# A recurrence step on VectorE as four whole instructions, and attention row transfers in another order on SyncE's queue

## The reference

```python
# layer 0, attention
scores = jnp.einsum('bhqd,bhkd->bhqk', q, k) / math.sqrt(HD)
attn = jax.nn.softmax(scores, axis=-1)
out = jnp.einsum('bhqk,bhkd->bhqd', attn, v)
# layer 1, the recurrence: one step for each token
def step(S, inp):
    q_t, k_t, v_t, g_t, b_t = inp
    S = S * jnp.exp(g_t)[..., None, None]
    mem = jnp.einsum('bhk,bhkv->bhv', k_t, S)
    delta = (v_t - mem) * b_t[..., None]
    S = S + jnp.einsum('bhk,bhv->bhkv', k_t, delta)
    o_t = jnp.einsum('bhk,bhkv->bhv', q_t, S)
    return (S, o_t)
```

## Time and profile before

| | us |
|---|---|
| median of 3 runs | 982.09 |
| lowest and highest | 980.87, 983.06 |
| profiled execution | 984.33 |
| its span in the trace | 982.5 |
| stretch of the attention groups in it | about 42 to 165 |
| steps of the recurrence in it | 544.4 to 679.3 |

### The profile page before, as it was taken

One profiled execution on the slowest core, in us unless ns is written; L12 is line 12 of the kernel. 1 busy time (PEld: TensorE's weight loads), 2 busy tenths in 40 slices (PEclk: granted clock), 3 DMA queues, 4 the chain that ended last, 5 costly groups with the idle time before them and its releaser, 6 DMA issues.

```text
span 982.5 us, 11403 instructions
## 1 busy us (share of the span) xinstructions
PE 780.4 (79%) x3600; PEld 508.9 (52%) x3600; DVE 636.3 (65%) x1522; ACT 287.5 (29%) x529; POOL 274.4 (28%) x250
## 2 busy tenths in 40 slices
PE   5876999879999999989503876453868699999983
PEld 4321333657777777744301322121345389999973
DVE  4785993654444444468998899998966734334335
ACT  2444776423334333335300543331011000000000
POOL 3630000211222222212744035334410124434410
PEclk9987999879999999999856887775978799999995
DMA  8691000001111111302200000000001289999945
GB/s 271 171 188 28 2 3 33 20 21 41 48 45 35 48 48 48 114 1 97 96 0 0 1 0 1 0 1 0 0 1 43 99 295 343 343 335 346 344 152 169
DMA packets 36405, 94.13 MB, mean 96 GB/s; under 512 B 4910, under 2 KB 17766, under 8 KB 35526
## 3 DMA queue, kind: packets, MB, share of 16 engines
q1 hardware_dynamic: 32262, 83.19, 26.4%
q0 software_dynamic: 3648, 9.97, 2.8%
q10 hardware_dynamic: 448, 0.39, 0.2%
HBM read 82.21 MB, written 12.12 MB: 96 GB/s over the span
## 4 chain that ended last, share of the span: by engine, by line
PE 54%; DVE 32%; issue 6%; DMA 5%; ACT 1%; SPq 1%; ACTq 0%; POOL 0%; DVEq 0%; POOLq 0%
PE psum L1243 14%; PE psum L1488 8%; PE psum L1498 7%; PE psum L1254 7%; DVE arena L1963 3%; DVE arena L1976 3%; PE psum L1143 3%; PE psum L1122 3%; PE psum L1132 3%; DVE arena L1954 2%; DVE arena L1967 2%; DVE small L1649 2%; DVE arena L309 2%; DVE arena L1923 2%; DMA max_scratch<-max_sb 1%
## 5 line engine op out<-in xcount | busy, mean ns | idle before, releaser
L1243 PE MATMUL psum<-xr,wr 128*128 128x512 f32 x600 | 159.3, 416 | 1.1 <-DVE arena L1798 1.1
L1243 PEld LDWEIGHTS psum<-xr,wr 128*128 128x128 f32 x600 | 116.3, 195 | 25.6 <-issue 1.3
L607 POOL TENSOR_TENSOR wr<-ring,wr 128x512 fp32r<-128x512 f32 (+1 forms) x50 | 54.3, 1105 | 198.9 <-ACT wr L810 198.9
L1649 DVE TENSOR_REDUCE small<-psum 128x1 f32<-128x512 f32 x128 | 80.9, 684 | 21.5 <-PE psum L1122 20.8
L1488 PEld LDWEIGHTS psum<-arena 128*128 128x128 f32 x700 | 83.3, 191 | 4.1 <-issue 1.6
L1488 PE MATMUL psum<-arena 128*128 128x128 f32 x700 | 84.0, 274 | 1.4 <-ACT arena L1010 1.1
L1498 PE MATMUL psum<-arena 128*128 128x256 f32 x350 | 81.8, 379 | 1.9 <-DVE arena L2162 1.9
L2151 DVE TENSOR_SCALAR arena<-psum,arena 128x256 f32<-128x256 f32 x35 | 16.9, 484 | 102.0 <-PE psum L1498 102.0
L1050 PE MATMUL psum<-sel,identb 128*128 128x512 bf16 x164 | 45.9, 421 | 46.2 <-DVE arena L1931 46.2
L1761 DVE TENSOR_TENSOR hid<-hid,psum 128x512 f32<-128x512 f32 x50 | 34.4, 688 | 69.0 <-ACT hid L816 69.0
L1254 PE MATMUL psum<-hr,wr 128*128 128x512 f32 x300 | 76.4, 391 | 0.2 <-DVE hr L1736 0.2
(11 more groups left out here) (364 smaller groups left out, 1339.2 us busy)
## 6 DMA issues: line engine op xcount, KB each, us to landing
arena<-in_w1u SPq DMA_DIRECT2D x35, 642.5 KB
arena<-in_w1d SPq DMA_DIRECT2D x35, 640.0 KB
ring<-in_w SPq DMA_DIRECT2D x25, 384.0 KB, 3.1
part_scratch<-arena SPq DMA_DIRECT2D x12, 256.0 KB, 2.0
arena<-z_scratch SPq DMA_DIRECT2D x8, 384.0 KB, 6.6
arena<-part_scratch SPq DMA_DIRECT2D x9, 256.0 KB, 12.9
qkv_scratch<-arena SPq DMA_DIRECT2D x4, 512.0 KB, 2.6
arena<-qkv_scratch SPq DMA_DIRECT2D x4, 512.0 KB, 4.0
```

The lines of the kernel that those rows point to most:

```text
L607: pool.tensor_tensor(wr0[:, k, LO, part], ring0[:, k, part], wr0[:, k, HI, part], ALU.subtract).then_inc(s["w0_lo"], 1)
L1243: ins = pe.matmul(bank[2 * b + m][:, :], wr0[:, k, w, lo:lo + P], xr[:, x, f, half(b)], start=(f == 0 and (w, x) == PARTS[0]), stop=(f == ...
L1649: dve.tensor_reduce(nm[:, g % 2, at16:at16 + 1], full("scores", n), AX, ALU.max, negate=True).then_inc(s["bank_free"], 1)
```

## The change

SyncE: row set 1 is issued ahead of the stores of pair 1 instead of behind them. Row set 3 is issued behind the maxima's two transfers of g = 1 instead of ahead of them. Row set 2 keeps its place behind the wait for pair 1. VectorE: each stage of a step is one instruction over both halves, with one semaphore `scan` instead of `scan_lo` and `scan_hi`; its count per step stays 4. The other engines wait for `scan` alone. The data, their places and the arithmetic of each element are the same.

```diff
             q_rows(sp, 0, half(1), rows_in(0, 1))
-            parts_out(1)
-            for t in range(1, NH // HG):
-                if t == 2:
-                    sp.wait_ge(s["parts_out1"], 16 * 6)
+            def all_rows(t):
                 k_rows(sp, t, slice(0, TOK), rows_in(t, 0))
                 q_rows(sp, t, slice(0, TOK), rows_in(t, 0))
+
+            all_rows(1)
+            parts_out(1)
+            sp.wait_ge(s["parts_out1"], 16 * 6)
+            all_rows(2)
...
                      max_dram.rearrange("(h j t) q -> h j (t q)", h=2, j=HG))
+                if g == 1:
+                    all_rows(3)
...
-                for x in range(2):
-                    if x == 0:
-                        dve.wait_ge(s["u_in"], n + 1)
-                    dve.wait_ge(own[x], 4 * n + 1)
-                    dve.tensor_reduce(fixed[:, x], pa[:, n % 2, x], AX, ALU.add).then_inc(own[x], 1)
...
+                dve.wait_ge(s["u_in"], n + 1)
+                dve.wait_ge(own, 4 * n + 1)
+                dve.tensor_reduce(fixed, pan, AX, ALU.add).then_inc(own, 1)
```

## The result

| | before | after |
|---|---|---|
| median of 5 runs each (us) | 982.09 | 991.71 |
| lowest to highest | 980.87 to 983.06 | 988.12 to 993.03 |
| profiled execution | 984.33 (span 982.5) | 991.71 (span 989.9) |
| TensorE's second scores of group 1 begin | 81.58 | 73.01 |
| the transposes behind attention begin (L1213, now L1214) | 166.65 | 159.30 |

The change made the kernel slower: the ratio after to before is 1.0095, with a 95% interval of 1.0073 to 1.0117. Both parts did what their diffs say, with opposite signs: attention and what follows it reach the recurrence 9.6 us earlier, the recurrence takes 19.4 us more, and 2.4 us come back behind it. That makes the 7.4 by which the spans differ. The medians differ by 9.6, because the profiled execution of before lay 2.2 above its median and that of after lies on it.

What follows compares the result with a forecast made beforehand. Neither PE (54% of the chain) nor DVE (32%) was taken to bound the whole kernel; VectorE sets the recurrence's time. Recurrence +23.0 - 4.3 = +18.7, attention -9.3, together +9.4 on 982.09: 991.5 us, range 977 to 1001.

Steps and rivals of the forecast that it cites:

- the main case: Whole kernel: recurrence +18.7 us, attention -9.3, so 991.5 us; chance 0.62.
- The plain step: Recurrence with GpSimd idle: a step takes 2.18 us instead of 1.82, +23.0 us for 64 steps.
- The waits for GpSimd: Recurrence beside GpSimd: VectorE's products wait 0.44 us each, 14.1 us in all instead of 18.4, so -4.3.
- The threshold: Recurrence beside GpSimd: GpSimd wants the memory again at 0.63 us, VectorE asks at 0.67, so GpSimd comes first.
- the first rival: Recurrence: GpSimd comes too late and VectorE never waits, +4.6 us there, kernel 977.4 us; chance 0.13.
- the second's: Recurrence: the gap is 0.04 before reduces too, VectorE asks at 0.60, ahead of GpSimd; kernel 968.5 us; chance 0.10.
- Attention: First exchange: the store of maxima lands right behind set 2, TensorE goes on at 72.7, -8.9 us; with clock -9.3.
- The lower bound of -11.9: Attention's largest gain: the store meets an empty queue, landing within about 1.4 us, and TensorE avoids the lower clock.
- TensorE's clock: Attention behind the wait: the shorter wait may spare TensorE the lower clock, a gain of 0 to 2.1 us, 0.4 taken.
- Row set 3: Attention: issued around 73 to 76, in by about 85; may delay the next exchange a us or so, costed at nothing.
- my own range: Whole kernel: the forecast's range, with L1955, attention and the waits at their bounds, 983 to 998 us.
- The third rival: Recurrence: a wait costs nothing, a step's four paces are 1.56 us, kernel 945.5 us; chance 0.03.

Runs made afterwards that it cites:

- the eleventh kernel: The changed kernel with each of GpSimd's products replaced by a write of one element; one run of 980.12 us.
- the fourth kernel: The changed kernel with the two waits in the other order ahead of both reduces; 985.31 us, ratio 1.0029.
- the fifth kernel: The changed kernel with each GpSimd product waiting for the one ahead and ScalarE's copies of sums and queries moved later; 982.08 us, ratio 0.9988.
- the second kernel: The kernel before with the whole instructions alone, SyncE's order as before; 999.44 us, ratio 1.0157.
- ninth kernel: The changed kernel with waits swapped ahead of both reduces, GpSimd's products made late, and the first 19 steps in halves; 966.88 us, ratio 0.9859.
- the eighth kernel: The kernel before with row set 1 alone moved ahead of the stores of pair 1; 979.33 us, ratio 0.9968.

## Why the prediction was right

The time came out at 991.71 for a forecast of 991.5, and the main case was the one that happened. By its steps:

- **The plain step** was 2.21 for 2.18. The reduces took 0.453 for 0.44, L1955 0.60 for 0.59, L1964 0.426 for 0.41; the gaps were 0.103 and 0.034 for 0.11 and 0.04. Over 64 steps that is +24.8 for +23.0. That the 0.11 belongs to the order of the two waits, and not to the copy from PSUM behind which it had been read, is shown by the two swaps.
- **The waits for GpSimd** were 154.2 - 64 x 2.208 = 12.9 us for 14.1 (12.5 by the eleventh kernel), the lengthening of a product 0.42 to 0.43 for 0.44. The recurrence as a whole came to 154.2 for about 153.
- **The threshold was the weak step.** "Wants the memory again at 0.63" was read from two record starts after GpSimd had come from idle. In a run of products the time is 0.57. The outcome was right, and safer than I thought: the margin was 0.10, not 0.04. But the first rival's price point was wrong, and so was the second's reasoning: with gaps of 0.04 everywhere VectorE would still have lost, at 985.3 (the fourth kernel) and not at 968.5. What that rival priced was reached only by making GpSimd late (966.4).
- **Attention** came at -8.6 for the wait, forecast -8.9, but by another road. The row sets were quicker than worked out: the six stores of pair 1 landed 0.6 us apart, the last one 1.1 behind the fifth, at 56.63 and not "by 60.9 at the latest", and set 2 was in at 66.93, not between 69 and 71.9. The store of maxima then met an idle queue, and by the prediction's own words it should have landed within 1.4. It took 3.05, with this in the windows (columns as in the next point):

```profile
68.00:69.00 1.00, 1.00 (x9) 0.33 (x10) 1.00 (x3) 0.54 (x2) 0.00 (x0) 1.00 0.10 24
69.00:70.00 1.00, 1.00 (x9) 0.11 (x2) 1.00 (x2) 0.77 (x1) 0.00 (x0) 1.00 0.00 1
```

  The 24 GB/s in the first of the two are the store's 8 KB and the 16 KB of the instruction packet. A store that waits for row loads and one whose last packets stand behind an instruction packet gave the same time by chance; the first was my mechanism, the second was what happened. The lower bound of -11.9, with a store of 1.4 and the clock kept, is the case of the fifth kernel, and it goes a little beyond: the second value matmuls end at 76.64 there, 12.7 earlier than before.
- **TensorE's clock** was forecast to give back 0.4 and took 0.9 instead: from TensorE's going on to the end of the second value matmuls it is 8.66 us, before 7.76. The granted clock is 0.50, the 1.2 GHz level, when TensorE goes on. The windows (start to end, length; busy us and count of PE, PEld, DVE, ACT, POOL; granted clock, DMA share, GB/s), first before, then after:

```profile
81.58:85.58 4.00, 4.00 (x15) 1.04 (x15) 1.98 (x3) 2.05 (x2) 0.00 (x0) 0.50 0.00 0
85.58:87.58 2.00, 2.00 (x14) 0.53 (x7) 0.69 (x1) 0.86 (x2) 0.00 (x0) 0.82 0.00 0
```

```profile
73.01:77.01 4.00, 4.00 (x15) 1.04 (x15) 1.98 (x3) 2.05 (x2) 0.00 (x0) 0.50 1.08 207
77.01:79.01 2.00, 2.00 (x11) 0.43 (x4) 0.41 (x1) 0.60 (x1) 0.00 (x0) 0.50 1.00 152
79.01:81.01 2.00, 2.00 (x10) 0.60 (x12) 1.78 (x5) 1.53 (x2) 0.00 (x0) 0.83 0.80 172
```

  Before, the full clock is back some 4.7 us after TensorE goes on, after the change some 6.7. The clock had fallen 8.9 us ahead of TensorE's going on before, and 0.16 ahead of it now, so that less of the slow stretch passed while TensorE was idle. The second value matmuls end at 88.29 + 1.05 before and 80.62 + 1.05 now, 7.7 earlier where the start was 8.6 earlier. At L1214 7.35 are left.
- **Two stretches with the same code** came out shorter in the profiled execution. The recurrence begins 9.6 earlier, 2.2 more than at L1214, and the stretch behind it gave 2.4 on top. The change made neither of them. From the transposes behind attention to the recurrence the 14 profiled executions take 375.5 to 379.2 us, those with SyncE's order of before 375.5 to 377.8. Behind the recurrence the 12 other kernels take 302.6 to 304.2, the second kernel with its whole instructions 302.6; the 300.9 of the changed kernel stands alone. So the first is scatter between single executions. The second lies 1.7 under the lowest of the others, over code that the change didn't touch, and most likely is scatter too; only one execution of the changed kernel has a trace. To cost both at nothing was right.
- **Row set 3** was issued from 71.65 and in by 82.17, 0.7 ahead of the next store of maxima at 82.87: it cost that exchange nothing that shows, as forecast. In the fourth, fifth and ninth kernel, where the first exchange is over earlier, the next store has row loads among its packets and takes 1.9 to 2.4 us; TensorE doesn't wait for it there either. GpSimd's memsets caused no wait in the rows read.
- **The range.** The low end of my own range, 983, doesn't follow from its terms: 991.5 - 5.8 - 2.6 - 1.3 is 981.8. The range that counts, 977 to 1001, doesn't hang on it.
- **The third rival**, free waits, is excluded by the 0.03 and 0.10 us behind every end. The Trainium skill, "VectorE: DVE Perf Modes", section "The DRAIN you can't avoid", has a semaphore at no cost; in this chain of single instructions the measurement says otherwise, and the measurement decides.

In sum, the parts came at +19.4 and -7.35, so +12.1 for a forecast of +9.4. The two stretches with the same code took 2.2 and 2.4 off that, which leaves +7.4 between the profiled executions. The medians differ by 9.6, since the profiled execution of before lay 2.2 above its median. So the forecast was hit within 0.2 because three errors nearly cancel: a sum 2.7 too small, 4.6 of scatter, and these 2.2. That closeness is luck. What the runs support is the mechanism of the recurrence, to within 1 us as a whole and 2 us in its two terms. Of attention they support that the row set ahead of the store held it back, and the size; what the store met in its place was not in the prediction.

## What to carry to other kernels

Splitting an instruction of a dependent chain in two, each half waiting for the instruction before the last, hides the tail and the semaphore's gap; merging them saves a fixed part but exposes both, here 0.39 us a step for four instructions. Where two engines take turns at one memory, read from the records who asks first and by how much: shifting one of them by a tenth of a microsecond was worth 14 us, twice what shortening the gaps of the chain brought. On a queue of transfers, look at what stands right ahead of the small transfer on the path, and move only that. A small transfer that is slow on an empty queue is worth a look at the packets of the other queues. And before a difference of 2 us in a stretch with the same code is put down to a change, the same stretch is worth reading in other profiled executions.

## What the runs showed of the hardware that I had not expected

- **Of two waits on an instruction, the order in the code has a price.** If the semaphore that comes last in time is the one that the code waits for last, the instruction starts 0.103 us after the end of the work it waits for; if the code waits for it first, 0.034. Two such swaps took 7.1 us off the recurrence (154.2 to 147.1).
- **A shift of 0.06 us decides who waits.** In the fourth kernel 27 products of VectorE begin 0.02 to 0.04 us behind a record of GpSimd, and each is 0.48 to 0.51 longer; in the fifth 49 begin up to 0.04 ahead of one, and none is longer by more than 0.01. The Trainium skill, "SBUF — State Buffer", section "Who interferes with whom", says that the order of issue decides who is blocked, and that products of two SBUF operands contend while reduces don't; the rows agree, with L1961 at 452/453/455 ns beside GpSimd and without it.
- **An 8 KB store on an idle queue takes 1.3 or 3 us and more.** In the changed kernel the stores of maxima took 3.05, 1.33, 3.3, 1.33, 3.4, 1.3 and 2.9 us, by turns. Each of the four slow ones has a 16 KB instruction packet among its own, and none of the fast ones.
- **A short wait brings TensorE's clock down as a long one does, and more of the work behind it can run at the lower level.** After 2.56 us of idleness the clock stayed at 0.50 for 6.7 us of TensorE's work, after 8.19 (the eighth kernel) for 4.1, after 10.72 for 4.7. After 0.83 us (fifth kernel) it never fell, nor after the 0.58 and 0.96 of the ninth and fourth:

```profile
71.15:73.15 2.00, 2.00 (x11) 0.73 (x15) 1.42 (x3) 1.36 (x2) 0.00 (x0) 1.00 0.97 209
```

  So what separates the two kinds of attention lies mostly at this one place. Against the changed kernel the fifth goes on 1.9 us earlier (71.15 for 73.01), and from there to the end of the second value matmuls it needs 5.5 us instead of 8.7.
